# Row adds, two layer norms and the context mean product behind the routed experts, as one pipeline over token tiles in one block

## The reference

```python
x = x + _L0_xattn_ref(_layernorm(x), ctx_1024, ...)     # 16 heads over 1601 context tokens
x = x + _L0_attn_ref(_layernorm(x), ...)                # self attention with rotary places
x = x + _L0_ffn_ref(_layernorm(x), ...)                 # shared SwiGLU + 8 routed experts, top 2
x = x + _L1_xattn_ref(_layernorm(x), ctx_1024, W, b)
x = x + _L1_attn_ref(_layernorm(x), ...)                # self attention, 8 heads, bias by distance
x = x + _L1_ffn_ref(_layernorm(x), ...)                 # 8 grouped matrix pairs

def _layernorm(x, eps=1e-05):                           # no weights
    return (x - mean(x)) / sqrt(var(x) + eps)

def _L1_xattn_ref(x1, x2, W, b):
    part1 = einsum('bld,ed->ble', x1, W[:, :256])
    part2 = einsum('bld,ed->be', x2, W[:, 256:]) / x2.shape[1]
    return part1 + part2[:, None, :] + b
```

## Time and profile before

| | us |
|---|---|
| median of 3 runs | 1342.28 |
| lowest, highest | 1341.74, 1342.65 |
| the profiled execution | 1330.97 |
| its span, first to last instruction | 1329.2 |

### The profile page before, as it was taken

How to read it: one execution, slowest core, us unless ns; L and a number is a source line. 1 busy time by engine, 2 the same in 40 slices (tenths; PEclk the granted TensorE clock), 3 DMA queues, 4 the chain that set the end, 5 groups by cost and what they waited for, 6 DMA issues and landing times. The chain is left out here.

```text
span 1329.2 us, 32322 instructions
## 1 busy us (share of the span) xinstructions
PE 1192.8 (90%) x13863; PEld 1048.1 (79%) x13863; DVE 709.3 (53%) x1127; ACT 556.1 (42%) x907; POOL 383.6 (29%) x339
## 2 busy tenths in 40 slices
PE   4799999999999999999999988796699999278799
PEld 4789889889889899899998977674477778266598
DVE  5555655565565575475475443275564222565732
ACT  4455555555555555555555532214532322111400
POOL 4632332332332342342242210053144000540000
PEclk9899999999999999999999985597989999589989
DMA  6937647647657556566665460190012121414045
GB/s 197 209 85 174 154 102 165 146 116 159 138 132 149 132 140 141 132 145 137 141 149 124 104 128 1 54 363 2 1 68 87 57 64 48 127 28 191 2 176 194
DMA packets 61732, 161.47 MB, mean 121 GB/s; under 512 B 24904, under 2 KB 38296, under 8 KB 58520
## 3 DMA queue, kind: packets, MB, share of 16 engines
q1 hardware_dynamic: 58904, 154.18, 46.0%
q0 software_dynamic: 1536, 4.20, 0.9%
q10 hardware_dynamic: 1152, 1.05, 0.2%
HBM read 70.56 MB, written 9.44 MB: 60 GB/s over the span
## 5 line engine op out<-in xcount | busy, mean ns | idle before, releaser
L366 ACT ACTIVATE xa_pt<-xa_sc 128x1024 f32<-128x1024 f32 (+1 forms) x224 | 212.4, 962 | 151.2 <-PE xa_sc L558 151.1
L412 DVE TENSOR_REDUCE xa_mx<-xa_sc 128x2 f32<-128x804 f32 x256 | 243.4, 991 | 41.4 <-PE xa_sc L542 41.4
L558 PE MATMUL xa_sc<-xa_queries,xa_keys 104*128 104x128 f32 (+1 forms) x1664 | 232.5, 285 | 2.4 <-DVE xa_queries L427 1.8
L558 PEld LDWEIGHTS xa_sc<-xa_queries,xa_keys 104*128 104x128 f32 (+1 forms) x1664 | 206.6, 196 | 21.0 <-issue 8.4
L479 PE MATMUL xa_pj<-xa_ctx_hi,xa_wk 128*128 128x400 f32 (+1 forms) x512 | 157.0, 349 | 0.9 <-DVE xa_qst L440 0.9
L479 PE MATMUL xa_pj<-xa_wv,xa_ctx_hi 128*128 128x256 f32 (+1 forms) x832 | 155.3, 286 | 0.1
L542 PE MATMUL xa_sc<-xa_keys,xa_queries 96*128 96x402 f32 x512 | 138.0, 373 | 13.0 <-DMA xa_keys<-xa_kst_hi 7.3
L569 PE MATMUL xa_op<-xa_pt,xa_values 128*32 128x64 f32 x6656 | 141.8, 228 | 7.7 <-ACT xa_pt L366 3.3
L295 POOL TENSOR_TENSOR xa_ctx_lo<-xa_raw,xa_ctx_hi 128x1600 fp32r<-128x1600 f32 (+1 forms) x32 | 115.9, 3623 | 78.0 <-DVE xa_ctx_hi L405 75.4
L300 POOL TENSOR_TENSOR xa_kst_lo<-xa_wk,xa_kst_hi 128x400 fp32r<-128x400 f32 x64 | 67.3, 1051 | 227.4 <-ACT xa_kst_hi L345 227.4
L479 PEld LDWEIGHTS xa_pj<-xa_wv,xa_ctx_hi 128*128 128x128 f32 (+1 forms) x832 | 126.2, 185 | 8.0 <-issue 6.5
(11 more groups left out here) (286 smaller groups left out, 1736.7 us busy)
## 6 DMA issues: line engine op xcount, KB each, us to landing
xa_keys<-xa_kst_hi SPq DMA_DIRECT2D x256, 200.2 KB, 6.1
xa_keys<-xa_kst_lo SPq DMA_DIRECT2D x128, 200.2 KB, 5.4
xa_raw<-in_ctxT SPq DMA_DIRECT2D x15, 1601.0 KB, 9.0
gf_w<-in_gf_w SPq DMA_DIRECT2D x16, 1024.0 KB, 7.1
moe_ex<-in_moe_ex SPq DMA_DIRECT2D x8, 1088.0 KB, 15.9
xa_queries<-xa_qst SPq DMA_DIRECT2D x96, 32.0 KB, 3.5
moe_slots_in<-in_moe_zero SPq DMA_DIRECT2D x1, 2944.0 KB, 16.4
moe_xs<-moe_slots_in SPq DMA_DIRECT2D x23, 128.0 KB, 2.2
```

The lines of the kernel that those rows point to most:

```text
L366: nc.scalar.activation(PT[ptslot(step)][0:rows, 0:nt], SC[bank(step)][0:rows, 0:nt], ACT.Exp, scale=float(D0) ** -0.5).then_inc(ex_done, 1)
L412: nc.vector.tensor_reduce(mx[:, u // 2, 2 * (u % 2):2 * (u % 2) + 2], SC[bank(step)][:, :, 0:MXN], AX.X, ALU.max).then_inc(mx_done, 1)
L558: last = mm(SC[bank(step)][0:rows, kk, a * P:(a + 1) * P], KS[:, 2 * a + h, kt * P:kt * P + rows], QS[b % 2][:, 2 * a + h, :], start=True, ...
```

## The change

One block does the work of four. `mean_context` and `context_means` go, and so do two of the calls of `layer_norm`; the last one, before the grouped products, is now number 3. At the end of `experts` every engine runs a loop over steps s = 0 to T + 1, in which tile s gets its row adds and first normalisation, tile s - 1 its product and context add, tile s - 2 its second normalisation. A tile's normalisation now is one root (`spread`), one inversion and one shift of a single column (`scales`), one ACT instruction x * rstd + shift (`normal`), two transpositions (`turn`) and one ACT copy (`evicted`). The context part is no longer a product with widened means: `from_means` takes one column of the mean as a stationary matrix of 64 equal columns, for two sequences side by side in the array (`tile_position`), and adds the bias by a product of one row of ones with the bias row. So for each tile it is four products of 64 stationary columns and one of a single row, where it was two products and a POOL add. `gathered` has a semaphore for each tile. The mc weights are loaded early in the block; the sb weights when the last routed product has been made, into the experts' weight space, in which the gf weights and those of sb now lie. An additional square root of eps loads ACT's table ahead of the loop.

```diff
@@ experts, SP @@
-            for dst, src, counted in last_experts:
+            for dst, src, counted in last_experts + mc_loads + row_load:
                 sp.dma_start(dst, src).then_inc(counted, 16)
...
+            sp.wait_ge(dn_full, nth("dn", NT - 1, 0))
+            for dst, src, counted in next_loads:
+                sp.dma_start(dst, src).then_inc(counted, 16)
@@ experts, PE @@
+            def from_means(t):
...
+                ge(pe, mc_read, t - 2)
+                for k in range(CH):
+                    for b in range(2):
+                        mm(MC[t % 3][b * S:(b + 1) * S, 0:D], mean1[:, k, 2 * t + b:2 * t + b + 1].to_broadcast([P, S]), mc_w["w2"][:, k, :],
+                           start=k == 0, stop=False, tile_position=(0, b * S))
+                mm(MC[t % 3][:, 0:D], ones[0:1, :], mc_row[0:1, :], start=False, stop=False)
+            def from_rows(t):
+                pe.wait_ge(turned_ev[0], t + 1)
+                for k in range(CH):
+                    last = mm(MC[t % 3][:, 0:D], XT[t % 2][:, k, :], mc_w["w1"][:, k, :], start=False, stop=k == CH - 1)
+                last.then_inc(mc_full, 1)
+            def turn(k, t):
+                pe.wait_ge(y_done[k], t + 1)
...
+                for q in range(CH):
+                    last = nc.tensor.transpose(LP[k][t % 2][:, q * P:(q + 1) * P], yt[k][t % 2][:, q * P:(q + 1) * P], c["ident"])
+                last.then_inc(turned[k], 1)
+            for t in range(2):
+                from_means(t)
+            for s in range(T + 2):
+                if 1 <= s <= T:
+                    from_rows(s - 1)
+                if s >= 2:
+                    turn(1, s - 2)
+                if s < T:
+                    turn(0, s)
+                if s + 2 < T:
+                    from_means(s + 2)
@@ experts, ACT @@
+            def spread(k, t):
+                act.wait_ge(var_done[k], t + 1)
+                nc.scalar.activation(std[k][:, t:t + 1], mv[k][:, t, 1:2], ACT.Sqrt, bias=eps[:]).then_inc(std_done[k], 1)
+            def normal(k, t):
+                act.wait_ge(scaled[k], 2 * t + 2)
+                ge(act, turned[k], t - 1)
+                nc.scalar.activation(yt[k][t % 2][:], X[:, t], ACT.Identity, bias=shift[k][:, t:t + 1], scale=rstd[k][:, t:t + 1]).then_inc(y_done[k], 1)
+            def evicted(k, t):
+                act.wait_ge(turned[k], t + 1)
...
+            for s in range(T + 2):
+                if 1 <= s <= T:
+                    evicted(0, s - 1)
+                if s < T:
+                    spread(0, s)
+                if s >= 2:
+                    normal(1, s - 2)
+                    evicted(1, s - 2)
+                if s < T:
+                    normal(0, s)
+                if 1 <= s <= T:
+                    spread(1, s - 1)
@@ experts, DVE @@
-            for t in range(T):
+            def adds(t):
                 dve.wait_ge(dn_read, T + t + 1)
-                if t % (T // NYG) == 0:
-                    dve.wait_ge(gathered[t * NYG // T], 16 * 2 * T // NYG)
+                dve.wait_ge(gathered[t], 16 * 2)
                 for k in range(2):
                     step_(V.scalar_tensor_tensor(X[:, t], back[2 * t + k], w2[:, k, t:t + 1], X[:, t], ALU.mult, ALU.add))
...
+            def context_add(t):
+                dve.wait_ge(mc_full, t + 1)
+                dve.wait_ge(y_done[0], t + 1)
+                V.tensor_tensor(X[:, t], X[:, t], MC[t % 3][:, 0:D], ALU.add).then_inc(mc_read, 1)
+                dve.wait_ge(mc_read, t + 1)
+                step_(V.bn_stats(st4[:, t], X[:, t]))
+                V.bn_aggr(mv[1][:, t], st4[:, t]).then_inc(var_done[1], 1)
+            for s in range(T + 2):
+                if s < T:
+                    adds(s)
+                if s >= 2:
+                    scales(1, s - 2)
+                if 1 <= s <= T:
+                    context_add(s - 1)
+                if s < T:
+                    scales(0, s)
```

More of the change, by code:

```diff
@@ L1109, in expert_order, with experts @@
     return o + down(1)
-def experts(nc, tag, X, y, stats, lnT, c, buffers, splits):
+def experts(nc, tag, X, y, stats, lnT, c, buffers, splits, tail):
     ctx = ExitStack()
@@ L1705, in program, with cut @@
         splits = shared_splits(nc, moe_stack, expert_parts, (ln["norm"], 3 * T))
+        def cut(at, **shapes):
+            parts = {}
+            for n, (k, m) in shapes.items():
+                parts[n] = ex[:, at:at + k * m].rearrange("p (k m) -> p k m", k=k)
+                at += k * m
+            return parts
+        gf_W = [cut(2 * WE * j, w1=(CH, FG), w2=(NF, D), b2=(1, D)) for j in range(NG)]
+        gf_W = [W | {"b2": W["b2"][:, 0]} for W in gf_W]
+        gf_in = [ctx.enter_context(nc.semaphore(f"gf_w_in{j}")) for j in range(NG)]
@@ L1739, in program @@
                        conv_bias=(a["sb_conv"], scratch), loads=gf_loads)
[L1741 removed]
+        layer_norm(nc, 3, ln, X, stats, lnT, c)
         grouped_ffn(nc, "gf", X, lnT, c, gf_dram, gf_W, gf_in, out)
```

128 lines of the change are left out of this document (58 added, 70 removed).

## The result

The changed kernel takes **1367.74 us** (median; 1367.06 to 1371.3 over four runs) where the kernel before takes 1342.1: the ratio is 1.0199, with a 95% interval of 1.0179 to 1.0218. I had forecast 1341.4 with a range of 1333.5 to 1350. It is 25.6 us slower, and both the number and its range are wrong.

A forecast was written before the change was run, and what follows sets the result against it. Bound first by gathers, then by whole-block dependences; the change leaves a closed ring. First context add 1136.82, five steps of 5.11, two of 4.21, tail 3.09, clock 7.2: 1181.1, 0.9 before the mark, so 1341.4 us; range 1333.5 to 1350.

The forecast's parts named there:

- closed ring: New tile loop: chain through DVE, ACT and PE from context add to context add, 5.11 us a tile at full clock.
- Rival E: New tile loop keeps the gathers' pace: 25 us less, 1317; chance 0.02.
- The ring's terms: Hand-overs and work of one loop step, from add to row products: 5.11 us at 2.4 GHz, 7.46 at 1.2.
- without means: Last two loop steps, which have no `from_means`: 4.21 us each at full clock, 5.32 at the low one.
- Rival C: In `from_means` the two column halves don't overlap on PE: 6.5 us more than the forecast, 1347.9; chance 0.06.
- The clock: TensorE's clock in the new loop goes up and down: 7.2 us added to an end at 1173.88.
- rival B: PE stays at 1.2 GHz through the loop: 6.2 us above the mark of 1181.98, 1348.5 in all; chance 0.26.
- two of the five full steps at the low one: Loop steps with means: two of five run at 1.2 GHz, adding 4.7 us.
- The first tile: Start of the new loop, shared adds to first context add: that add at 1136.82, 10.95 us after the first gather.
- transposition to copy 0.44: Hand-over from PE's transposition to ACT's copy of the turned tile: 0.44 us at full clock, hidden behind `from_means`.
- The bridge from trace to runs: Whole kernel: the gain of 0.9 us from the trace taken off the runs' median, 1342.28, giving 1341.4.
- The edits at nothing: Early mc and sb loads, context sum, mean scaling, table load, semaphore clears: no cost, bounds 0 and about 2 us.

The follow-up runs named there:

- e8_warm: The changed kernel with four useless products more in each pass of PE from s = 2 on, between the two turns: 1353.2 us, ratio 1.0101.
- e4_paced: The changed kernel with one wait more on POOL: a tile's two gathers are issued only when the previous tile's have landed: 1352.4 us, ratio 1.0082.
- e9_no_means_once: The changed kernel with the scales and normal steps moved ahead, gathers paced by landing, scatters broken in fours, from_means as in the change: 1323.1 us, ratio 0.9879.
- e7_all_fours: The changed kernel with means multiplied once for all sequences, gathers paced by landing, scales and normal moved ahead, scatters broken in fours: 1323.5 us, ratio 0.9883.
- e5_order: The changed kernel with VectorE's scales ahead of the previous tile's context add and ScalarE's normal ahead of the copy to lnT: 1339.3 us, ratio 0.9994.
- e10_gather_fours: Same as e7_all_fours, but with the break in the gathers behind each second tile (four gathers) instead of each tile: 1320.0 us, ratio 0.9849.

## Why the prediction was wrong

**What bounds the kernel.** Right: the tiles pass at the pace of a closed ring, not of the gathers; every context add waited for the row products. Rival E, the gathers' pace, was rightly put low.

**The ring's terms.** Right within 0.4 us a step: 7.87 for 7.46 at the low clock (my own terms add up to 7.48), 5.26 for 5.11 at the high one, 5.35 for 5.32 and 4.16 for 4.21 without means. Two terms were too small at both clocks: `normal`, 0.66 up to PE for 0.54 (it took 0.60 itself, between my bounds of 0.38 and 0.76), and the two transpositions, 0.62 for 0.50 at the low clock and 0.37 for 0.24 at the high one (1178.30 to 1178.67 in e8_warm). At the low clock means (3.05 for 2.92) and row products (2.11 for 2.03) make up the rest. Rival C is refuted: the two column halves do run side by side.

**The clock.** The step that failed second. I let it go up and down, and took rival B, low throughout, at 0.26. It was low from 1151 to the end of the stretch. It fell there before the hole, behind PE's wait of 2.28 us ahead of the first transposition, and the hole, in which PE did almost nothing for ten us, could not bring it back. But the ring lets it fall by itself: in e4_paced, without the hole, the clock was full for the first tile, fell at 1155.8, behind the first wait of 2.12 us, and never came back. The step that failed is thus "two of the five full steps at the low one": all five were, in e4_paced the first of them from its middle on. The rule of the Trainium skill that I weighed there (TensorE: Matmul & The Clock Gate, Part 4, PE-mode transpose: transpositions don't count as PE's being busy in the same way) spoke for B, and the low clock agrees with it; I had let a pair of rows from another place outweigh it. e8_warm fits the gap and the rule alike, since it fills the gap with products, so whether transpositions count is left open; e9_no_means_once, with the same four in each tile, has the full clock. By rival B the time would have been 1348.5, inside my range.

**The first tile.** The step that failed first, and the larger one. The hand-overs from PE were taken as constants, from rows at which no indirect transfer was going on: "transposition to copy 0.44", hidden behind the means, and the shared adds on time at 1130.89. The transposition to the copy took 13.27 us (1150.60 to 1163.87), 12.8 of them behind the transposition's end. The last shared adds had been idle for 3.03 us instead of 1.39 for the same reason. Together that is most of the 14.5 by which the first context add is late, at 25.45 for 10.95. Without it (e4_paced) the changed kernel takes 1352.4: 3.9 above rival B and still 2.4 above my range. They stand in the stretch (66.1 for 62.3): 2.2 up to the first context add, most of it because the shared adds end 1.9 later behind the first gather in that execution, and 1.6 in ring and tail.

**The bridge from trace to runs.** The profiled execution was 11.3 us below the median of the runs, and I carried that gap along as a constant, without asking what it was. Most of it was this effect, among the scatters. A gap of 0.8%, where the three runs agreed within 0.1% among themselves, was the one clue in sight. The later runs of the kernel before spread wider, from 1335.4 to 1344.0, but none comes near 1331.

**The edits at nothing.** The semaphore clears cost nothing, though they did not stand where I put them: in time they ran beside the gathers, not behind them. The first pair of gathers, beside the sb loads, was 2.6 us late in e4_paced, covered there by the shared adds; in the change the late signal to those adds hides it.

**What stays open.** An unbroken stream of POOL's indirect transfers is shown to be needed for the late signals: breaks take them away at two places, in both kernels. It is not sufficient, since one profiled execution with sixteen scatters and sixteen gathers in a row had none. The late increment is recorded only at 1163.85, 0.02 before ScalarE starts, so it is held before it counts, and not by ScalarE. Where, and why from PE, while ScalarE's at 1150.55 reached PE by 1150.60 in the same stream, was not tried.

A rival that no run here tests is the recording itself. Sixteen indirect transfers mark their landing 256 times. The execution of the earlier trace rows, which had unbroken rows of them and no late signal, has all 256 marks in its trace, for the scatters and for the gathers. Every other trace lacks some: 57 to 81 are left in an unbroken row of scatters, 34 to 56 in one of gathers, 115 to 179 with a break behind each fourth, 219 to 254 behind each second, and increments by the engines themselves are missing there too. Some of those traces have no late signal all the same (e7_all_fours). Lost records and late signals may have one cause, or taking the trace may be part of it; whether the signals are late in an execution of which no trace is taken is not shown.

## What to carry to other kernels

When a trace is quicker than the runs, find out what it lacks before anything is summed on it. A pipeline of small hand-overs is only as good as its slowest signal: before engines are made to hand tiles around beside a stream of indirect transfers, try a break in the stream, a wait for its own landing every few transfers, even if the transfers get slower. And look for the order that closes a ring: moving one step of VectorE and one of ScalarE ahead of a wait was worth more (23.9 us of the stretch) than shortening that ring's largest term (11.7, of which 2.2 are a shorter hole), and TensorE's clock came up with it.

## What the runs showed of the hardware

- Signals of PE came late in ten of the eleven traces in which sixteen indirect transfers of POOL follow each other 1.25 us apart without a break: up to 12.8 us, for a hand-over of 0.03 to 0.05 otherwise. With a break of 1.7 to 4.6 us behind each second or fourth transfer they came on time at the places that matter here.
- TensorE's clock stayed at 1.2 GHz through fifty us of a ring in which PE was busy 18.91 of 24 us, much of it transpositions and column-tiled products with 1.7 us of waiting in a step. Where the ring began at 2.4 GHz (e4_paced), the clock fell in its first step. It rose to 2.4 GHz when products without use filled that wait (e8_warm), or when the ring was opened (e5_order).
- PE was busy for 27.74 of 30.70 us in e10_gather_fours and had 1.2 GHz, for 17.12 of 20 in e5_order and had 2.4. The first has four transpositions and a product over 16 rows in each tile beside the row products, the second ten records of means and bias in place of that product's two. Why the first stayed low is open.
- With column-tiled products, two halves of 64 columns ran side by side though they share the moving matrix and the stationary one is a repeated column: eight records of 256 columns took 1.01 us up to the next product in e8_warm (1178.67 to 1179.68), where full-width ones come every 0.215.
